# Spectra of a four-layer convolution kernel: how the first layer's bands are reordered between two blocks

## The reference, cut to what matters

```python
def _L0_conv_ref(x, weights_r, weights_i):          # first layer
    w = (weights_r + 1j * weights_i)
    x_ft = jnp.fft.rfft2(x)
    out_ft = zeros                                  # 4 bands of 8 rows x 16 columns are kept
    mix = lambda xs, ws: jnp.einsum('bixy,ioxy->boxy', xs, ws)
    out_ft[:, :, :8, :16]    = mix(x_ft[:, :, :8, :16], w[0])
    out_ft[:, :, 50:58, :16] = mix(x_ft[:, :, 50:58, :16], w[1])
    out_ft[:, :, 56:, :16]   = mix(x_ft[:, :, 56:, :16], w[2])
    out_ft[:, :, 6:14, :16]  = mix(x_ft[:, :, 6:14, :16], w[3])   # later bands overwrite earlier ones
    return irfft2(out_ft)
...
def _L2_conv_ref(x, weight):                        # third layer: 5x5 filter, 32 to 32 channels, reflect padding
...
x = x + _L0_conv_ref(_gn(x), L0_conv_weights_r, L0_conv_weights_i)
x = x + _L1_conv_ref(_gn(x), L1_conv_gain)
x = x + _L2_conv_ref(_gn(x), L2_conv_weight)
x = x + _L3_conv_ref(_gn(x), L3_conv_weights)
```

## Time and profile before

| What | us |
|---|---|
| median of 3 runs | 879.6 (875.92 to 885.77) |
| the profiled execution | 882.25 |
| its span (first to last instruction) | 880.4 |
| forward stage of the first layer, first products to the last group's copies | 150 to 204.5 |
| its block ends with SP's last load; the next starts on DVE | 212.13 |
| the mix stage's first product | 214.50 |
| the inverse stage's first instruction on TensorE | 240.9 |

### The profile page before, as it was taken

The page is one execution under the profiler, slowest core; times in us unless marked ns, Lnnn a source line. Parts: engine busy times, 40 slices in busy tenths (PEclk is TensorE's granted clock), DMA queues, the critical chain, the costliest instruction groups (busy, mean ns, idle before and its releaser), DMA issues. The chain is left out here.

```text
span 880.4 us, 27840 instructions
## 1 busy us (share of the span) xinstructions
PE 735.8 (84%) x11781; PEld 623.0 (71%) x11781; DVE 576.8 (66%) x1074; ACT 420.7 (48%) x727; POOL 120.0 (14%) x119
## 2 busy tenths in 40 slices
PE   7999997882588558785899999958999488879997
PEld 7999997882577337674444444428998488879997
DVE  3554452885849656887777777777775867746454
ACT  0132334782454006553699995004778267754200
POOL 0000001440000004552022313004320100000000
PEclk9999998996979668987999999987999699999995
DMA  8599987764020000000000000004000478830055
GB/s 312 197 369 322 338 247 223 165 139 113 6 55 3 1 1 2 0 0 0 2 1 2 1 1 1 1 1 96 2 2 8 90 158 177 175 64 1 2 193 194
DMA packets 48686, 80.70 MB, mean 92 GB/s; under 512 B 20162, under 2 KB 38472, under 8 KB 43736
## 3 DMA queue, kind: packets, MB, share of 16 engines
q1 hardware_dynamic: 31960, 62.65, 25.6%
q10 hardware_dynamic: 16640, 16.78, 5.6%
HBM read 50.91 MB, written 27.92 MB: 90 GB/s over the span
## 5 line engine op out<-in xcount | busy, mean ns | idle before, releaser
L1587 DVE SCALAR_TENSOR_TENSOR X<-bank,c_power,X 32x512 f32 x128 | 96.7, 755 | 36.5 <-PE bank L1537 32.9
L1738 PE MATMUL bank<-m_xp,m_kf 128*32 128x64 f32 x2048 | 82.8, 248 | 23.4 <-DVE m_xp L1673 11.1
L1738 PEld LDWEIGHTS bank<-m_xp,m_kf 128*32 128x32 f32 x2048 | 81.8, 171 | 24.5 <-issue 24.4
L421 DVE COPY ks_rows<-bank 128x512 f32<-128x512 f32 x64 | 41.2, 687 | 66.4 <-PE bank L351 66.4
L221 DVE BATCH_NORM_STATS2 bn<-X 128x6 f32 (+1 forms) x128 | 81.2, 682 | 2.9 <-POOL X L1327 1.6
L439 ACT COPY ks_spec<-bank 128x512 f32<-128x512 f32 x64 | 34.3, 589 | 93.8 <-PE bank L366 93.8
L1493 ACT ACTIVATE c_r<-X,c_nrm 32x1024 f32 (+1 forms) x56 | 75.0, 1340 | 2.4 <-DVE c_nrm L1561 1.1
L351 PE MATMUL bank<-ks_fw,ks_src 64*128 64x64 f32 x1024 | 68.7, 298 | 6.4 <-DMA ks_src<-in_L_conv_weights 6.4
L587 POOL TENSOR_SCALAR f_src<-X,rstd,shift 128x512 f32<-128x512 f32 x52 | 40.2, 776 | 238.2 <-POOLq L243 200.7
L351 PEld LDWEIGHTS bank<-ks_fw,ks_src 64*128 64x128 f32 x1024 | 68.1, 215 | 6.3 <-issue 6.3
L366 PE MATMUL bank<-ks_fh,ks_rows 64*128 64x128 f32 (+1 forms) x1152 | 71.2, 278 | 0.0
(11 more groups left out here) (181 smaller groups left out, 1658.6 us busy)
## 6 DMA issues: line engine op xcount, KB each, us to landing
ks_src<-in_L_conv_weights SPq DMA_DIRECT2D x16, 1024.0 KB, 7.1
kf<-ks_spec ACTq DMA_DIRECT2D x16, 1024.0 KB, 8.7
m_kf<-kf SPq DMA_DIRECT2D x32, 512.0 KB, 7.9
X<-in_x SPq DMA_DIRECT2D x4, 2048.0 KB, 13.1
out_y<-X SPq DMA_DIRECT2D x32, 256.0 KB, 2.6
xf<-l_y SPq DMA_DIRECT2D x24, 112.0 KB, 2.1
l_wb<-in_L_conv_weights_r SPq DMA_DIRECT2D x4, 512.0 KB, 11.7
l_wb<-in_L_conv_weights_i SPq DMA_DIRECT2D x4, 512.0 KB, 13.7
```

The lines of the kernel that those rows point to most:

```text
L421: dve.tensor_copy(rows[p][:, m, :, C // 2 * g + r:C // 2 * (g + 1):2], ps[2 * g + r][:].rearrange("p (c n) -> p n c", n=N)).then_inc(rows_ ...
L1587: dve.scalar_tensor_tensor(x, of.rearrange("p (y x) -> p y x", x=HN), filt.power[at, 2:3], x, ALU.mult, ALU.add).then_inc(added, 1)
L1738: last = pe.matmul(ps[4 * half + m // 8][at:at + C, m % 8 * N:(m % 8 + 1) * N], kf[p][:, j, :, H * half + m], xp[half][:, j, m].rearrange( ...
```

## The change

Groups 0 to 2: each part is stored to `xf` by one transfer from all 128 partitions, its destination walked in the order k, c, and each band is loaded by one transfer of 64 partitions for both parts; so two stores and four loads a group, and the counts waited for are changed to fit. The last group's 32 copies are numbered by band, part and k; ACT takes 0 to 10, DVE 11 to 23, POOL 24 to 31. The third layer's filter is still scaled and split by DVE (`split`); DVE then lays out `high` and ACT `low`.

```diff
@@ -678,42 +678,37 @@
                 for q in range(Q - 1):
                     sp.wait_ge(negated, S * q + S)
                     for part in range(2):
-                        for k in range(4):
-                            sp.dma_start(pr.xf[q, part, :, S * k:S * k + S].rearrange("c k n -> c (k n)"),
-                                         xm[q % 2][k * C:(k + 1) * C, part].rearrange("p s k r b -> p (s k r b)")
-                                         ).then_inc(moved[q % 2], 16)
-                    sp.wait_ge(moved[q % 2], 128 * (q // 2) + 128)
+                        sp.dma_start(pr.xf[q, part].rearrange("c (k s) n -> k c (s n)", k=4),
+                                     xm[q % 2][:, part].rearrange("p s k r b -> p (s k r b)")).then_inc(moved[q % 2], 16)
+                    sp.wait_ge(moved[q % 2], 32 * (q // 2) + 32)
                     for w in range(4):
-                        for part in range(2):
-                            to = (w % 2 * 2 + part) * C
-                            n = len(L0_BLOCKS[w])
-                            sp.dma_start(xb[to:to + C, w // 2, q, :, 0:n].rearrange("c k x r b -> c k (x r b)"),
-                                         pr.xf[q, part, :, :, L0_OFF[w] * 2 * IB:(L0_OFF[w] + n) * 2 * IB]
-                                         ).then_inc(xb_loaded, 16)
+                        to = w % 2 * 2 * C
+                        n = len(L0_BLOCKS[w])
+                        sp.dma_start(xb[to:to + 2 * C, w // 2, q, :, 0:n].rearrange("c k x r b -> c k (x r b)"),
+                                     pr.xf[q].rearrange("t c k n -> (t c) k n")[
+                                         :, :, L0_OFF[w] * 2 * IB:(L0_OFF[w] + n) * 2 * IB]).then_inc(xb_loaded, 16)
 
             @block.tensor
             def _(pe):
                 filt.spread_largest(pe)
                 fwd.products(pe)
 
-            def last_group(eng, copy, blocks):
+            def last_group(eng, copy, pieces):
 
                 eng.wait_ge(negated, S * Q)
-                for w in blocks:
+                for piece in pieces:
+                    w, part, k = piece // 8, piece // 4 % 2, piece % 4
                     n = len(L0_BLOCKS[w])
-                    for part in range(2):
-                        to = (w % 2 * 2 + part) * C
-                        for k in range(4):
-                            copy(xb[to:to + C, w // 2, Q - 1, S * k:S * k + S, 0:n].rearrange(
-                                "c s x r b -> c s (x r b)"),
-                                xm[(Q - 1) % 2][k * C:(k + 1) * C, part, :, L0_OFF[w]:L0_OFF[w] + n].rearrange(
-                                    "c s x r b -> c s (x r b)"))
+                    to = (w % 2 * 2 + part) * C
+                    copy(xb[to:to + C, w // 2, Q - 1, S * k:S * k + S, 0:n].rearrange("c s x r b -> c s (x r b)"),
+                         xm[(Q - 1) % 2][k * C:(k + 1) * C, part, :, L0_OFF[w]:L0_OFF[w] + n].rearrange(
+                             "c s x r b -> c s (x r b)"))
 
             @block.scalar
             def _(act):
                 def keep(q, s, bank):
                     if s == 0 and q >= 2:
-                        act.wait_ge(moved[q % 2], 128 * (q // 2))
+                        act.wait_ge(moved[q % 2], 32 * (q // 2))
                     if s == 0 and q == 0:
                         for p in range(2):
                             act.wait_ge(pr.kf_stored[p], START + 16 * (C // IB))
@@ -722,13 +717,13 @@
                     return act.copy(xm[q % 2][:, 1, s, :, 1, :], made[:, :, 0, :])
 
                 fwd.high_parts(act, keep)
-                last_group(act, act.copy, (0, 1))
+                last_group(act, act.copy, range(0, 11))
 
             @block.vector
             def _(dve):
                 filt.find_power(dve)
                 fwd.low_parts(dve)
-                last_group(dve, dve.tensor_copy, (2, 3))
+                last_group(dve, dve.tensor_copy, range(11, 24))
 
             @block.gpsimd
             def _(pool):
@@ -742,6 +737,7 @@
                         pool.tensor_tensor(xm[q % 2][:, 1, i, :, 0, :],
                                            pr.zero[:].unsqueeze(2).broadcast_to([P, KX, IB]),
                                            xm[q % 2][:, 0, i, :, 1, :], ALU.subtract).then_inc(negated, 1)
+                last_group(pool, pool.tensor_copy, range(24, 32))
 
 
 
@@ -763,7 +759,7 @@
             @block.tensor
             def _(pe):
                 pe.wait_ge(w_loaded, 16 * 8)
-                pe.wait_ge(xb_loaded, 16 * 8 * (Q - 1))
+                pe.wait_ge(xb_loaded, 16 * 4 * (Q - 1))
                 for t in range(KT // 4):
 
                     for n in range(PAIR):
@@ -789,7 +785,9 @@
 
             @block.vector
             def _(dve):
-                filt.lay_out(dve, scaled, parts, seq)
+                filt.split(dve, scaled, parts, seq)
+                dve.wait_ge(seq, 2)
+                filt.lay_out(dve.tensor_copy, filt.high, parts[0])
                 for p in range(2):
                     dve.wait_ge(pr.kf_stored[p], START + 16 * (C // IB))
                 for t in range(KT // 4):
@@ -798,6 +796,8 @@
 
             @block.scalar
             def _(act):
+                act.wait_ge(seq, 3)
+                filt.lay_out(act.copy, filt.low, parts[1])
                 for p in range(2):
                     act.wait_ge(pr.kf_stored[p], START + 16 * (C // IB))
                 for t in range(KT // 4):
@@ -1395,7 +1395,7 @@
         dve.tensor_scalar(power[:, 2:3], power[:, 1:2], 1.0 / (W_UP * X_UP), None, ALU.mult)
         dve.reciprocal(power[:, 3:4], power[:, 1:2])
 
-    def lay_out(self, dve, scaled, parts, seq):
+    def split(self, dve, scaled, parts, seq):
 
         flat = "p o y -> p (o y)"
         dve.tensor_scalar(scaled[:].rearrange(flat), self.raw[:].rearrange(flat), self.power[:, 3:4], W_UP,
@@ -1405,19 +1405,18 @@
         dve.wait_ge(seq, 2)
         dve.tensor_tensor(parts[1][:].rearrange(flat), scaled[:].rearrange(flat), parts[0][:].rearrange(flat),
                           ALU.subtract).then_inc(seq, 1)
-        dve.wait_ge(seq, 3)
+
+    def lay_out(self, copy, to, of):
 
         def taps(d):
 
             k = [k for k in range(3) if 0 <= d + 2 * k < KS]
             return slice(k[0], k[-1] + 1), slice(d + 2 * k[0], d + 2 * k[-1] + 1, 2)
 
-        for to, of in zip((self.high, self.low), parts):
-            for ry, cx, oy, ox in np.ndindex(2, 2, 2, 2):
-                at = slice((2 * ry + cx) * C, (2 * ry + cx + 1) * C)
-                (ky, jy), (kx, jx) = taps(oy - ry), taps(ox - cx)
-                dve.tensor_copy(to[at, ky, kx, 2 * oy + ox, :],
-                                of[at].rearrange("c o (y x) -> c y x o", x=KS)[:, jy, jx, :])
+        for ry, cx, oy, ox in np.ndindex(2, 2, 2, 2):
+            at = slice((2 * ry + cx) * C, (2 * ry + cx + 1) * C)
+            (ky, jy), (kx, jx) = taps(oy - ry), taps(ox - cx)
+            copy(to[at, ky, kx, 2 * oy + ox, :], of[at].rearrange("c o (y x) -> c y x o", x=KS)[:, jy, jx, :])
 
 
 def l2_stage(pr, filt):
```

## The result

The changed kernel takes 899.16 us (median of six executions, 889.28 to 913.14) against 882.68 us (875.35 to 886.02) for the kernel before on the same chip. The ratio is 1.015, with a 95% interval of 1.009 to 1.021: slower by 8.3 to 18.2 us. In the profiled execution (912.44 us) the last stage, far behind the change, is longer too (mean of the L1052 products 400 ns, 303 before). I therefore quote it for the first layer's stage alone, where a second profile of the same kernel (891.24 us, experiment 5) has the same times within 0.6 us.

What follows compares the result with a forecast made beforehand. SP's DMA queue, setting when the last `xb` transfer lands, was taken to bound the first layer's stage. TensorE's start, 197.4 + 3T = 227.7 with T = 10.1, is 13.2 us later; 879.6 + 13.2 gives 893 us, range 884 to 907.

Steps and rivals of the forecast that it cites:

- Four engines, not sixteen: Stores to `xf`: the destination's outermost count of 4 leaves four DMA engines working, the other twelve standing still.
- The moving time T: Time four engines need for a group's 917,504 B of stores to `xf`: 10.1 us at 22.8 GB/s each.
- the third rival: Stores to `xf` by four engines at the loads' rate: T = 8.8, 9.3 us later, 889 us; 0.14 including less queueing.
- the sum: TensorE's start in the first layer's stage: 197.4 + 3T = 227.7, 13.2 us later than 214.50.
- The +6.6 us: TensorE's delay by the same sum with the skill page's rate, about 27 GiB/s per engine, T 7.9 us.
- Stores behind loads: SP's queue: the next group's stores wait behind the loads, landing 6.1 + T + 0.6 us after the previous group's.
- The loads: Four loads to `xb`, all sixteen engines, 0.63 us an issue: 7.2 us from issue to TensorE's start, against 8.3.
- The waits of ACT: ACT's waits on landed stores: no stall at group 2, 7.4 us at group 3, all hidden by SP.
- Copies and lay-out: Last group's copies on three engines and filter lay-out shared with ACT: worth nothing.
- The sixteen-engine case: Stores to `xf` spread over all engines, T = 3.6 us: TensorE at 208.9, 5.6 us gained, 874 us; chance 0.14.

Runs made afterwards that it cites:

- experiment 5: The changed kernel run once more with no edit, against the kernel before: 894.63 us, ratio 1.023.
- row_order: Changed kernel with its two stores landing in partition order, outermost count 128 in place of 4 (first layer computes something else): 875.22 us, 0.996 of the kernel before.
- outer_two: Changed kernel with four stores of 64 partitions a group, outermost count 2, in place of two of 128: 913.6 us, 1.040 of the kernel before.
- experiment 4: Changed kernel with the old eight stores a group, keeping its merged loads, copies and lay-out: 876.86 us, 0.999 of the kernel before.
- only_copies: Also 6: kernel before plus only the last group's copies on three engines and the filter lay-out by DVE and ACT: 879.3 us, ratio 0.995.
- step_in_psum: Also 9: changed kernel with channel-first partitions for 128-row stores, step of four in the transposes' PSUM writes: 874.28 us, 0.993 of the kernel before.
- step_in_psum_old: Also 10: as step_in_psum, but last group's copies on ACT and DVE and the whole lay-out on DVE: 881.1 us, 0.993 of the kernel before.
- four_stores: Changed kernel with four stores a group, one per k with both parts, outermost count 32: 880.7 us, 0.995 of the kernel before.
- four_again: The kernel of four_stores run again, unedited, beside step_in_psum on one chip: 875.9 us, 0.996 of the kernel before.

## Why the prediction was right

The kernel was slower by the mechanism forecast, and by nearly its size: 13.2 us forecast for TensorE's start, 14.46 measured; a ratio of 893 / 879.6 = 1.015 forecast, 1.015 measured. Point by point:

**Four engines, not sixteen.** Right, and shown by undoing it alone (`row_order`) and by making it worse alone (`outer_two`). The Trainium skill's rule in "DMA: Bandwidth & Descriptors", section "Why a DMA increments its semaphore by 16 and not by 1", gave the engines of 128, 4 and 2 right in all three cases.

**The moving time T.** The term was mis-sized, and two errors nearly cancelled; that 13.2 us came within 1.3 us of the measured time is in part luck. I took the rate of the output stores, 22.8 GB/s an engine, T = 10.1 us. The engines did 26 GB/s once running, as the loads at the start, so T = 8.8: the third rival's rate, which I had given little because no store of that trace reached it. Three times 1.3 us are 3.9 us less than forecast. Against that, the stores started slowly: 48 GB/s from 177 to 181 us at a share of 0.24, so the four engines were occupied but moved half as much. In the records of single packets one of 3,584 B takes 140 ns once running, but many of the first take 250 to 1,060 ns, and the four engines don't recover together: from 187 to 188 us the share is 0.12, two of them. Group 0's stores took 13.91 us for the 11.8 forecast, and by the true rate 10.5: 3.4 us more. From group 0's landing to group 1's were 16.63 us, where the sum at 26 GB/s gives 6.1 + 8.8 + 0.6 = 15.5: 1.1 more. To group 2's were 15.59, as that sum gives. With 0.3 us in the last loads and 0.2 in the first issue: -3.9 + 3.4 + 1.1 + 0.3 + 0.2 = +1.1 us, against 228.96 - 227.7 = 1.3 found. The Trainium skill's rate in "DMA: Bandwidth & Descriptors", section "Specifications", about 27 GiB/s (29 GB/s), lies about as far above the measured 26 as my 22.8 lay below. The +6.6 us that it gave was 7.9 us short: 2.7 for the rate (three times 0.9), 4.5 for the slow starts, the rest in small terms. What makes the first stores slow wasn't tried and stays open. The loads of the products' weights, issued before 155, had left the engines by about 172, so they are not it; nor is the place in the stage alone, for `row_order`'s first packets, at the same place, took 143 ns on average.

**Stores behind loads.** Right: the digits show it, and the interval of 15.59 us holds only with it. Alone, group 2's stores would have landed 10.5 us after their issue at 208.98, at 219.5; SP went on at 221.44.

**The loads.** 7.52 us from the issue of group 2's first load to TensorE's start, 7.2 forecast; an issue of 1,024 rows took a median of 678 ns, 0.63 us taken. What I had not counted is that the joined loads free SP at every group, worth 2.9 us of the stage with good stores (experiment 4 against 6). The four-engine stores hid it.

**The waits of ACT.** 7.87 us at group 3, 7.4 forecast. At group 2, 1.46 us where I had none, because group 0's stores came 2.3 us later than in my sum. Both were hidden, as said: the last group was copied by 213.02, and SP issued group 2's loads at 221.44 (220.5 forecast).

**Copies and lay-out.** Worth nothing, as forecast: `only_copies` and the pair 9 and 10 show it with slow and with fast transfers. POOL's copy took 0.44 us, within 0.37 to 0.77, and ACT's lay-out 7.54 us, within 5.6 to 10.4. It ended 6.6 us after TensorE's start, within 4.2 to 9.0; the wait that followed before the last quarter was TensorE's to end, 3.60 us for ACT and 3.20 for DVE.

**The rivals.** The sixteen-engine case is what `row_order` and `step_in_psum` are. It had TensorE at 208.9, and they have 208.73 and 209.71. But in it the arithmetic sets the pace again: SP comes to group 2's stores at 196.95 in `row_order`, right when group 2 is negated. Of the 5.6 us that were to be gained, `step_in_psum` shows 4.8 at the first product and a ratio of 0.993.

## What to carry to other kernels

Joining transfers to save issues is a gain only if the joined transfer still offers all engines a share: look at the outermost count of both sides, the side that is walked in another order above all. The share of the DMA engines over a stretch with that transfer alone tells it at once (here 0.57, 0.25, 0.13 for counts 128, 4, 2). If an order must be changed on the way, put the step where it is free: here it cost twelve of sixteen engines in a store's destination, some 90 to 125% more time for ACT's and DVE's writes, and nothing in the PSUM writes of a transpose.

## What the runs showed that was not expected

**A store from all 128 partitions uses the engines better.** `row_order`'s two stores need 2.4 us of fully used engines for 917,504 B (24.7 GB/s each); the four stores of 32 partitions run at 15.6 GB/s an engine in the first group, and the eight old ones at 16.3. The sixteen-engine rival had taken the old 3.6 us.

**Four engines are not slower each for being alone or for sharing.** 26 GB/s an engine with four at work, 26.5 with two, 26.0 with sixteen on the loads.

**A stage's length may vary with no edit in it.** From TensorE's first product to the next stage, taken to the first issue on SP there, the thirteen profiles have 26.25 to 29.01 us; `four_stores` had 29.01 and `four_again`, the same kernel, 26.25. The difference lies in pauses of TensorE between runs of 128 products, put down to issue: 0.98 to 1.44 us in the changed kernel, 0.67 to 1.70 in `step_in_psum_old`. In all thirteen profiles a DMA packet of 16,384 B of the kind `instruction` lands 1.2 to 1.6 us before the products go on after each pause: the later it lands, the longer the pause. So TensorE seems to wait there for its next instructions; no run tests it. The pauses blur the whole time by more than some of the edits do.

**The last stage scatters more than any edit here gains.** Its 1,024 products (L1052 in the changed kernel), the same in all thirteen profiles, keep TensorE busy for 29.9 to 53.2 us, 271 to 406 ns each. The two profiles of the changed kernel differ by 21.2 us in span and by 22.2 us in these products, over which the granted clock was 0.57 in one (849 to 905 us) and 1.00 in the other (849 to 884 us). That is why the argument goes by the first layer's stage.
